# An attention and bilinear block on one core: psi and one weight split move earlier in batch 0, the eight `s8` scalings go, `br` keeps two copies

## The reference, cut to what matters

```python
# block 0
q = einsum('bcn,dc->bnd', x1, Wq) + bq                 # d = 64
k = einsum('bcn,dc->bdn', x2, Wk) + bk[:, None]
v = einsum('bcn,dc->bdn', x2, Wv) + bv[:, None]
attn = softmax(einsum('bnd,bdm->bnm', q, k), axis=2)
x = einsum('bcm,bnm->bcn', v, attn) + x1
# block 1, x_2 is the same context
g_x, theta_x, phi_x = conv1x1(g, x_2).T, conv1x1(theta, x).T, conv1x1(phi, x_2)
W = einsum('bnc,bcm->bnm', theta_x, phi_x) / 1024
y = einsum('bnm,bmc->bnc', W, g_x).transpose(0, 2, 1)
out = bn(conv1x1(w, y)) + x
```

## Time and profile before

| | |
|---|---|
| Time of three runs, us | 1046.45 median (1045.68 to 1046.81) |
| Profiled execution: time, span, us | 1046.45, 1044.6 |
| PE busy, of the span | 1028.4 us (98%), 5055 matmuls |
| PEld, DVE, ACT, POOL busy, us | 851.5, 688.3, 492.6, 296.2 |
| Mean DMA rate | 117 GB/s |
| Batch 0, batch 1, the seven later ones, us | to 148, 148 to 275.6, about 127.6 each and 130.9 for the last |

### The profile page before, as it was taken

How to read it: one execution, slowest core, us unless ns; L and a number is a source line. 1 busy time by engine, 2 the same in 40 slices (tenths; PEclk the granted TensorE clock), 3 DMA queues, 4 the chain that set the end, 5 groups by cost and what they waited for, 6 DMA issues and landing times.

```text
span 1044.6 us, 13876 instructions
## 1 busy us (share of the span) xinstructions
PE 1028.4 (98%) x5055; PEld 851.5 (82%) x5055; DVE 688.3 (66%) x970; ACT 492.6 (47%) x835; POOL 296.2 (28%) x253
## 2 busy tenths in 40 slices
PE   8979999999999999999999999999999999999998
PEld 6768887888878888888888888888887888878887
DVE  6976287853788447884488735887367863688625
ACT  7643265533654246443555426443275432755321
POOL 1651152112611227012270123601245012530220
PEclk9989999999999999999999999999999999999999
DMA  7525352252613515146142452424423344333412
GB/s 253 156 56 137 121 185 68 71 148 100 217 39 79 179 74 196 46 101 195 61 163 58 109 177 71 152 66 112 166 91 131 78 108 159 120 102 81 129 34 81
DMA packets 80916, 121.94 MB, mean 117 GB/s; under 512 B 13136, under 2 KB 46800, under 8 KB 80848
## 3 DMA queue, kind: packets, MB, share of 16 engines
q1 hardware_dynamic: 71632, 104.26, 32.6%
q10 hardware_dynamic: 9216, 16.78, 5.1%
HBM read 70.66 MB, written 16.78 MB: 84 GB/s over the span
## 4 chain that ended last, share of the span: by engine, by line
PE 83%; DVE 9%; ACT 3%; issue 2%; POOL 2%; SPq 1%; DMA 1%; ACTq 0%; DVEq 0%; POOLq 0%
PE pG L654 31%; PE pG L560 11%; PE pG L665 8%; PE pG L568 5%; PE pG L599 5%; PE pT L687 4%; PE pG L687 4%; PE pG L575 4%; DVE acc L904 3%; PE pS L611 2%; DVE pT L924 2%; PE pM L633 2%; PE pT L611 2%; PE pM L642 2%; ACT x2Ts L785 2%
## 5 line engine op out<-in xcount | busy, mean ns | idle before, releaser
L654 PE MATMUL pG<-pt,vT 128*128 128x512 f32 x1536 | 354.1, 389 | 1.1 <-DVE pt L986 1.1
L654 PEld LDWEIGHTS pG<-pt,vT 128*128 128x128 f32 x1536 | 286.8, 188 | 60.0 <-issue 1.4
L1093 POOL TENSOR_TENSOR xms<-xr,xms 128x512 fp32r<-128x512 f32 x64 | 89.4, 1398 | 327.0 <-ACT xms L845 327.0
L560 PE MATMUL pG<-wv,x2s 128*128 128x512 f32 x720 | 169.1, 392 | 1.1 <-DVE vT L937 0.5
L560 PEld LDWEIGHTS pG<-wv,x2s 128*128 128x128 f32 x720 | 133.9, 188 | 32.5 <-issue 2.5
L1009 DVE SCALAR_TENSOR_TENSOR xr<-pG,cl,xr 128x512 f32<-128x512 f32 x64 | 47.8, 748 | 170.4 <-PE pG L654 170.4
L845 ACT ACTIVATE xms<-xr 128x512 fp32r<-128x512 f32 x64 | 40.2, 629 | 178.2 <-DVE xr L1009 178.2
L986 DVE TENSOR_TENSOR pt<-mv,pt 128x512 fp32r<-128x512 f32 x128 | 91.9, 768 | 39.6 <-ACT pt L825 39.3
L1089 POOL TENSOR_TENSOR ys<-yf,ys 128x256 fp32r<-128x256 f32 x32 | 29.6, 927 | 282.6 <-ACT ys L816 282.6
L1064 POOL TENSOR_TENSOR x2Ts<-x2T_f,x2Ts 128x512 fp32r<-128x512 f32 x64 | 83.9, 1338 | 48.9 <-ACT x2Ts L785 48.9
L825 ACT ACTIVATE pt<-mv 128x512 fp32r<-128x512 f32 x128 | 71.7, 620 | 39.5 <-PE pM L642 31.6
(11 more groups left out here) (145 smaller groups left out, 1478.9 us busy)
## 6 DMA issues: line engine op xcount, KB each, us to landing
mv<-tp SPq DMA_DIRECT2D x512, 64.0 KB, 2.0
x2T_f<-in_ctx2T_dram SPq DMA_DIRECT2D x32, 512.0 KB, 4.8
xr<-in_x_dram ACTq DMA_DIRECT2D x64, 256.0 KB, 4.2
st<-in_ctx_dram SPq DMA_DIRECT2D x31, 512.0 KB, 5.8
st<-in_x_dram SPq DMA_DIRECT2D x29, 512.0 KB, 4.1
out_dram<-oh SPq DMA_DIRECT2D x32, 256.0 KB, 2.0
out_dram<-xr SPq DMA_DIRECT2D x31, 256.0 KB, 7.4
x_raw<-in_x_dram SPq DMA_DIRECT2D x3, 512.0 KB, 8.0
```

The lines of the kernel that those rows point to most:

```text
L560: last = mm(bank, x2s[:, l, c, 128 * m:128 * m + 128], wv[:, r, c, :], start=(c == 0 and n == 0), stop=(c == 3 and n == 2))
L654: last = mm(bank, vT[:, l, m, 128 * c:128 * c + 128], pt(h)[:, r, m, :], start=(m == 0 and n == 0), stop=(m == 7 and n == 2))
L1093: done(tt(xms(h)[:, c, LO, :], xr[c][:, :], xms(h)[:, c, HI, :].bitcast(F), ALU.subtract), "xlo")
```

## The change

In batch 0 PE runs psi before Y:0 instead of between S:7 and Y:3, and ACT splits `wo` (`w:8`) between Y:0 and Y:1 instead of after S:7. Row `br` is twice as wide: columns 0 to 255 keep the bias as loaded, 256 to 511 take it times 8. `do_Y` reads the plain half with `scol`, and `do_s8`, `scol8` and their waits are gone; DVE's first Y waits for the load of `br` instead. The small tiles lose the 640 bytes of padding and the assertion. `br` is 1024 bytes longer, `scol8` was 32, so every tile from `ra` on begins 1024 - 32 - 640 = 352 bytes further, at an odd multiple of 32 bytes where it was a multiple of 64.

```diff
 FIRST = dict(
     pe=(
-        "GT:1 v:7 S:5 Y:0 Y:1 Y:2 S:6 S:7 psi Y:3 PV:0,0,0 PV:0,1,0 M:0 M:1 ...
+        "GT:1 v:7 S:5 psi Y:0 Y:1 Y:2 S:6 S:7 Y:3 PV:0,0,0 PV:0,1,0 M:0 M:1 ...
     act=(
-        "... T:2 S:5 T:3 Y:0 Y:1 Y:2 S:6 Y:3 psi S:7 w:8 xr:0 "
+        "... T:2 S:5 T:3 Y:0 w:8 Y:1 Y:2 S:6 Y:3 psi S:7 xr:0 "
...
-        br = at("br", [128, 256], F, o); o += 1024
+        br = at("br", [128, 512], F, o); o += 2048
...
-        scol8 = at("scol8", [128, 4], F, o); o += 32
...
-        o += 640
-        assert (o - base) % 512 == 0
...
-            eng.dma_start(br[:, :], brow[0:256].partition_broadcast(128)).then_inc(s_bd, 16)
+            eng.dma_start(br[:, 0:256], brow[0:256].partition_broadcast(128)).then_inc(s_bd, 16)
...
             def do_Y(b, c):
                 wait(eng, "g", b, G_Y + c)
-                if c == 0:
-                    wait(eng, "s8", b)
-                done(stt(out=yf[:, c, :], in0=br[:, :], scalar=scol8[:, c:c + 1], in1=bank_of(G_Y + c)[:, 0:256],
+                if b == 0 and c == 0:
+                    eng.wait_ge(s_bd, 16)
+                done(stt(out=yf[:, c, :], in0=br[:, 0:256], scalar=scol[:, c:c + 1], in1=bank_of(G_Y + c)[:, 0:256],
...
-            def do_s8(b):
-                wait(eng, "x2sum", b, 3)
-                done(eng.tensor_scalar(scol8[:, :], scol[:, :], 128.0 / N, None, ALU.mult), "s8")
...
-                eng.tensor_scalar(br[:, :], br[:, :], N / 128.0, None, ALU.mult).then_inc(s_br8, 1)
+                eng.tensor_scalar(br[:, 256:512], br[:, 0:256], N / 128.0, None, ALU.mult).then_inc(s_br8, 1)
```

More of the change, by code:

```diff
@@ L28 @@
     x2sum=4, x2lo=4, oa=4,
-    x2Tlo=8, s8=1, acc=8, acclo=1, Ylo=4, xlo=8, x1lo=8,
+    x2Tlo=8, acc=8, acclo=1, Ylo=4, xlo=8, x1lo=8,
 )
@@ L85 @@
     pool=(
-        "x2T:0 x2T:1 x2T:2 x2T:3 x2T:4 x2T:5 x2T:6 x2T:7 acc s8 Y:0 Y:1 Y:2 Y:3 PV:0,0 PV:0,1 PV:0,2 PV:0,3 PV:1,0 "
+        "x2T:0 x2T:1 x2T:2 x2T:3 x2T:4 x2T:5 x2T:6 x2T:7 acc Y:0 Y:1 Y:2 Y:3 PV:0,0 PV:0,1 PV:0,2 PV:0,3 PV:1,0 "
         "PV:1,1 PV:1,2 PV:1,3"
@@ L112 @@
     pool=(
-        "x1:0,0 x1:0,1 x1:1,0 x1:1,1 x1:2,0 x1:2,1 x1:3,0 x1:3,1 s8 x2T:0 x2T:1 x2T:2 x2T:3 x2T:4 x2T:5 x2T:6 "
+        "x1:0,0 x1:0,1 x1:1,0 x1:1,1 x1:2,0 x1:2,1 x1:3,0 x1:3,1 x2T:0 x2T:1 x2T:2 x2T:3 x2T:4 x2T:5 x2T:6 "
         "x2T:7 Y:0 Y:1 Y:2 Y:3 PV:0,0 PV:0,1 PV:0,2 PV:0,3 PV:1,0 PV:1,1 PV:1,2 PV:1,3"
@@ L904, in do_acc @@
                     done(stt(out=acc(b)[:, :], in0=wpg[:, part, c, 0:256].bitcast(F), scalar=scol[:, c:c + 1],
-                             in1=acc(b)[:, :] if n else br[:, :], op0=ALU.mult, op1=ALU.add), "acc")
+                             in1=acc(b)[:, :] if n else br[:, 256:512], op0=ALU.mult, op1=ALU.add), "acc")
             def do_accl(b):
@@ L1082, in do_acc @@
                     eng.wait_ge(s_accp, n + 1)
-                    done(tt(acc(b)[:, :], accp[:, :], acc(b)[:, :] if n else br[:, :], ALU.add), "acc")
+                    done(tt(acc(b)[:, :], accp[:, :], acc(b)[:, :] if n else br[:, 256:512], ALU.add), "acc")
                 wait(eng, "acchi", b)
@@ L1093, in do_PV @@
                 done(tt(xms(h)[:, c, LO, :], xr[c][:, :], xms(h)[:, c, HI, :].bitcast(F), ALU.subtract), "xlo")
-            do = dict(x1=do_x1, x2T=do_x2T, s8=do_s8, acc=do_acc, Y=do_Y, PV=do_PV)
+            do = dict(x1=do_x1, x2T=do_x2T, acc=do_acc, Y=do_Y, PV=do_PV)
             eng.memset(ecol[:, 4:8], -0.5).then_inc(s_id, 1)
```

## The result

The changed kernel takes 1052.77 us (median of 4 runs, 1052.42 to 1054.65), the kernel before beside it 1046.63 (4 runs, 1045.68 to 1047.06). The ratio is 1.0063 with a 95% interval of 1.0046 to 1.0081, so it is slower, by 6.1 us between the medians. The forecast was 1044.9, in a range of 1044.1 to 1046.8. The profiled execution took 1052.06 us, its span 1050.3.

What follows compares the result with a forecast made beforehand. PE was taken as the bound, busy 1028.4 of 1044.6 us. Psi's -0.34 and the `wo` split's -1.21 sum to -1.55 us from 1046.45, giving 1044.9 us, range 1044.1 to 1046.8.

Steps and rivals of the forecast that it cites:

- 352 bytes: Tiles behind the small ones start 352 bytes further; claimed no change in time, with the cost otherwise left to rival 4.
- rival 4: DVE and ACT slow down on shifted tiles in later batches; at 5% 2.8 us slower, 1049.2 us; chance 0.11.
- Psi, -0.34: Batch 0: psi runs in PE's wait before Y:0, so PE is 0.34 us earlier from Y:3; bounds 0.24 and 0.50.
- The split of `wo`, -1.21: Batch 0: ACT's earlier split brings mt and T:7 forward, removing PE's wait before PV:1,0,0; 1.21 us won, bounds 0 and 1.21.
- Rival 1: Batch 0: POOL's subtraction holds up DVE's second half of T:7, 1.09 us later; gain only 0.7, 1045.7 us; chance 0.12.
- Rival 2: Batch 0: PE's clock rises sooner with psi, 0.68 us more won, 1044.2 us; chance 0.10.
- Rival 3: Batch 0: the wait at 104 before PV:1,0,0 stays, only psi's 0.34 comes through, 1046.1 us; chance 0.12.
- `s8`, `br`, `scol`: Eight POOL instructions of 243 ns go; claimed 0 won, at most 1.9 us if all lay on the path.

Runs made afterwards that it cites:

- order alone: The kernel before with only the two moves of batch 0, all addresses as before: 1045.81 us against 1046.80, ratio 0.9992.
- psi alone: The kernel before with only psi moved ahead of Y:0, the split of `wo` left behind S:7: 1046.89 us, ratio 1.0003.
- distance kept: The changed kernel with its seven small tiles, 352 bytes together, placed ahead of the weights: 1045.73 us against 1047.05 for the kernel before, ratio 0.9989.
- all + 352: The kernel before with every tile, weights too, 352 bytes further: 1046.99 us, ratio 0.9999.

## Why the prediction was wrong, step by step

**352 bytes: the step that failed.** The prediction wrote "No row shows a big tile at such a start ... so I take no change", and put the bounds of that term on DVE and ACT alone (rival 4). The term is 1.29 us of PE's pace per batch, 1.06 net of the waits that it swallows, 7.4 us in seven batches and 0.4 in batch 0 (theta and B there). Rival 4 had the place right, the shift, and the mechanism wrong. Its rows in batch 2 of the changed kernel, against the earlier trace rows:

```profile
276.10 0.48 DVE L901 SCALAR_TENSOR_TENSOR acc<-wpg,scol,br 128x256 f32<-128x256 f32 x1
...
287.67 0.67 DVE L934 TENSOR_TENSOR vT<-pG,vT 128x512 fp32r<-128x512 f32 x1
```

Neither is longer by more than 0.01 us, and from the one to the other are 11.57 us in both kernels. The engine with 98% of the span was the one for which the question was not asked: a cost of 3% on those matmuls is paid in full, while most of DVE's work has slack to fall into. The shift should have been priced against the earlier trace rows first: what does each per cent on the matmuls with one moved operand cost? They are 188 of the 632 of a batch (k and q 16 each, v 96, theta 48, B 12), and 1% of 188 x 0.2267 us in seven batches is 3.0 us. With that bound the upper end of the range would have been higher. The prediction took the lines of 16 bytes from the Trainium skill ("SBUF — State Buffer", "Specifications (TRN2)") and worked out from them that whole lines have no effect. For DVE and ACT the trace agrees (busy 688.3 and 492.6 us before, 687.6 and 492.7 after); for PE's two operands the measurement decides, and there is an effect.

**Psi, -0.34.** It ran inside the wait (64.52, done before 65.92), as forecast, but the term was too large. PE's timeline from S:6's first matmul to PV:0,0,0, before:

```profile
72.25 0.50 PE L611 MATMUL pS<-khi,qhi 64*128 64x512 f32 x2
...
75.60 5.63 PE L654 MATMUL pG<-pt,vT 128*128 128x512 f32 x24
```

and changed:

```profile
71.73 0.50 PE L608 MATMUL pS<-khi,qhi 64*128 64x512 f32 x2
...
74.84 5.61 PE L651 MATMUL pG<-pt,vT 128*128 128x512 f32 x24
```

That is 3.35 us before and 3.11 changed, and 3.11 with the order alone, psi alone and the distance kept too. So psi is worth 0.24, the lower bound: the 0.34 between the starts of psi and Y:3 leave out that Y:3's twelve take 1.52 from start to start behind the scores, where they took 1.43 behind psi. Y:0's start scatters by more than that (66.35, 65.92, 67.36, 67.73 and 66.20 in the profiles of before, changed, order alone, psi alone, distance kept), so the gain is seen in the traces and not in the times.

**The split of `wo`, -1.21.** Held: 71.16 on ACT, no idle on DVE, mt at 83.36, T:7 on ACT at 98.83 (forecast 98.9), the wait gone; 1.26 us by the difference of the two kernels above. In batch 0 of the changed kernel Y:0 was 0.43 us early, Y's first 36 matmuls took 0.09 less, and psi gave 0.24; with the 1.21, and less 0.40 for theta's and B's pace, that is 1.57, and batch 1 is 1.61 earlier. That this is near the forecast 1.55 is luck: the first two belong to the scatter of Y:0's start and of the clock, and the pace takes 0.40. The two moves themselves make 1.45 in the trace. The forecast sum of -1.55 is answered by -1.0 [-1.8, +0.1] for the order alone and -1.3 [-2.1, -0.2] with the distance kept.

**Rival 1** did not come. POOL's subtraction at 101.30 took 1.60 us where it had taken 1.28, and T:7's two halves took 1.28 together: DVE was first, and its second half ended at 101.75. The rule that the prediction quotes from the Trainium skill ("SBUF — State Buffer", "SBUF: two separate sides") has POOL wait until then, 0.45 us; its instruction was 0.32 longer, so the rule fits to about 0.1 us. **Rival 2** did not come: PE was at the high clock from 69.0, 3.1 us after Y:0 at 65.92, and 3.1 us after it before. With the order alone and with the distance kept it rose at 72.1, 4.7 and 5.9 us after Y:0. So psi brought nothing forward in any of them, and that the changed kernel came near the forecast 69.4 is luck. **Rival 3** did not come; psi alone shows what it would look like. **`s8`, `br`, `scol`** are worth nothing, as forecast: with the distance kept, batches are 127.64 to 127.70 apart, before 127.61.

## What to carry to other kernels

When a change moves tiles in SBUF, by a padding, a widened row or a dropped tile, write down for each group of matmuls how the distance between the starts of its two operands changes. Where PE is the bound, keep it at a multiple of 256 bytes, as it is in the kernel before, whose weights and big tiles all start at multiples of 512 from the base. These runs show it for matmuls like these alone. Compare the start-to-start pace of each matmul group in the traces, not only the waits. A term for which no row exists needs its bounds on the engine that bounds the kernel first. And price a step that is moved away by the time between its two neighbours, with and without it: the next group can take up a part of the gap.

## What the runs showed of the hardware that was not expected

**The distance of two operands.** The matmuls of theta, k, q, v and B, of 512 columns in fp32r, start 0.2267 us apart when the start of the streamed tile is 0 or 256 bytes from its old distance to the loaded one, and about 0.233 at 32, 96 (352) or 128; at 64 (320) it is 0.2288 where the weights are loaded and 0.233 where they are streamed. The absolute start did not matter in the one shift tried (all + 352). Matmuls of 256 columns answer in another way: M's 12 take 1.43 us at 0 and at 352, 1.40 at 32, 1.41 at 64 and 1.45 at 128. Y's 36, start to start, take 4.41 us at 0, 4.42 at 352, 4.37 or 4.38 at 32 and 128, and at 64 mostly 4.20 us, 5% less. So the distance that costs the wide matmuls most need not cost the narrow ones. What in the reads meets is open, and so is why the two roles differ at 64. v's pace is read from its 24; its 60 take 0.12 or 0.13 us more than 60 such steps (13.73 us from start to start at 0, 14.15 at 352), whatever the distance.

**When the low clock comes and goes.** In batch 0 all profiles have a stretch at 1.2 GHz, but it moves from execution to execution. PE's granted clock in the kernel with the distance kept (window, length, busy and count, clock, DMA share, GB/s):

```profile
62.00:62.20 0.20, 0.00 (x0) 0.50 0.21 46
69.00:69.40 0.40, 0.40 (x4) 0.50 0.00 0
...
72.20:72.40 0.20, 0.20 (x4) 1.00 0.00 0
```

Here it is low from 62.0 or earlier to 72.1, before from about 62.7 to 69.5, with the order alone from 65.3 to 72.1. Y's 36 matmuls take 7.14, 5.96 and 6.63 us in the three. That is nearly as much as the forecast gain, so a single time can't show such a gain; that it makes the scatter of the ten runs too is not shown.
